# A two-layer graph kernel on one core: the half tile's first product dealt among the wide matmuls of the tile in front, and the unit numbers loaded three at a time

## The reference

```
x = x + C @ (D^-1/2 (sym(adj) + I) D^-1/2) @ layernorm(x)     # graph layer: C is adj too
h = layernorm(layernorm(x)) * gamma + beta                    # 2048 tokens of 512
shared = silu(h @ q(sw1).T) @ q(sw2).T                        # 512 -> 1024 -> 512
e, p = argmax and max of softmax(h @ router.T)                # one expert of 8 for each token
routed = p * (silu(h @ q(ew1[e]).T) @ q(ew2[e]).T)
x = x + shared + routed
```

## Time and profile before

| | |
|---|---|
| times of three runs | 663.97, 664.15, 666.87 us (median 664.15) |
| the profiled execution | 665.43 us, of which the span is 663.7 us |
| mean granted PE clock | 0.991 |
| PE busy | 615.6 us (93%), 4713 matmuls |
| DVE busy | 478.0 us (72%) |
| ACT busy | 371.7 us (56%) |
| POOL busy | 185.8 us (28%) |
| chain that ended last | PE 64%, DMA 13%, DVE 12%, issue 5%, ACT 4% |

### The profile page before, as it was taken

How to read it: one execution, slowest core, us unless ns; L and a number is a source line. 1 busy time by engine, 2 the same in 40 slices (tenths; PEclk the granted TensorE clock), 3 DMA queues, 4 the chain that set the end, 5 groups by cost and what they waited for, 6 DMA issues and landing times.

```text
span 663.7 us, 14071 instructions
## 1 busy us (share of the span) xinstructions
PE 615.6 (93%) x4713; PEld 348.9 (53%) x4713; DVE 478.0 (72%) x1075; ACT 371.7 (56%) x699; POOL 185.8 (28%) x222
## 2 busy tenths in 40 slices
PE   0689899999997999999997999999999999999994
PEld 0234344444443444444443467777766666676672
DVE  4888986777776655778866669887885677666764
ACT  1667756677887777688836513556633424334241
POOL 2234343322210100202232416100120544445432
PEclk9999999999999999999998999999999999999998
DMA  8999990795878888967675975998259589676651
GB/s 341 420 416 415 421 368 26 187 225 144 233 230 259 292 263 274 351 226 254 206 237 203 225 209 129 236 227 178 78 90 231 148 192 183 180 193 173 181 127 62
DMA packets 105971, 149.87 MB, mean 226 GB/s; under 512 B 64590, under 2 KB 64590, under 8 KB 101808
## 3 DMA queue, kind: packets, MB, share of 16 engines
q1 hardware_dynamic: 91280, 116.82, 58.5%
q0 software_dynamic: 7632, 23.23, 11.3%
q10 hardware_dynamic: 6992, 8.93, 4.5%
HBM read 117.73 MB, written 18.25 MB: 205 GB/s over the span
## 4 chain that ended last, share of the span: by engine, by line
PE 64%; DMA 13%; DVE 12%; issue 5%; ACT 4%; SPq 1%; POOL 1%; DVEq 0%; ACTq 0%; POOLq 0%
PE bank L1785 14%; PE bank L1813 13%; PE bank L1680 10%; PE bank L1678 10%; PE bank L1679 10%; DMA region<-in_adj_t 7%; DMA work<-in_w 3%; PE bank L1828 2%; ACT junk L940 2%; DVE region L1194 2%; PE bank L1842 1%; DMA hb<-h_scratch,zreg 1%; PE bank L1708 1%; DVE region L1190 1%; DVE work L1308 1%
## 5 line engine op out<-in xcount | busy, mean ns | idle before, releaser
L1813 PE MATMUL bank<-region,work 128*128 128x512 f16 (+1 forms) x512 | 116.8, 379 | 3.5 <-DVE work L1466 3.3
L1049 ACT ACTIVATE work<-work 128x512 f32<-128x512 f32 x64 | 39.8, 621 | 108.0 <-DVE work L1456 107.4
L1678 PE MATMUL bank<-region,work 128*128 128x512 f16 x192 | 73.7, 384 | 26.4 <-DVE region L1218 26.3
L1813 PEld LDWEIGHTS bank<-region,work 128*128 128x128 f16 x512 | 46.6, 98 | 61.3 <-issue 9.1
L1785 PE MATMUL bank<-zreg,region 128*128 128x128 f16 x1280 | 75.7, 219 | 0.0
L1785 PEld LDWEIGHTS bank<-zreg,region 128*128 128x128 f16 (+1 forms) x1280 | 72.7, 98 | 3.7 <-issue 0.2
L1679 PE MATMUL bank<-region,work 128*128 128x512 f16 x192 | 73.5, 383 | 0.0
L1680 PE MATMUL bank<-region,work 128*128 128x512 f16 x192 | 73.5, 383 | 0.0
L1678 PE MATMUL bank<-zreg,work 128*128 128x512 f16 x180 | 69.6, 386 | 0.0
L1680 PE MATMUL bank<-zreg,work 128*128 128x512 f16 x180 | 69.5, 386 | 0.0
L1679 PE MATMUL bank<-zreg,work 128*128 128x512 f16 x180 | 69.5, 386 | 0.0
(11 more groups left out here) (211 smaller groups left out, 1160.4 us busy)
## 6 DMA issues: line engine op xcount, KB each, us to landing
work<-in_w SPq DMA_DIRECT2D x46, 512.0 KB, 4.5
region<-in_adj SPq DMA_DIRECT2D x16, 1024.0 KB, 10.7
region<-in_adj_t SPq DMA_DIRECT2D x16, 1024.0 KB, 7.7
work<-in_adj_t SPq DMA_DIRECT2D x32, 384.0 KB, 4.4
region<-in_w SPq DMA_DIRECT2D x12, 512.0 KB, 4.2
xb<-in_w SPq DMA_DIRECT2D x10, 512.0 KB, 4.3
zreg<-s_scratch SPq DMA_DIRECT2D x17, 256.0 KB, 3.9
zreg<-in_x SPq DMA_DIRECT2D x4, 1024.0 KB, 9.7
```

What stands on the lines that cost most here:

```text
L1049: nc.scalar.activation(h1[:, cols], pre[:, cols], ACT.Silu).then_inc(h1_ok, 1)
L1678: nc.tensor.matmul(dst, a_hi, b_hi, start=start, stop=False, skip_group_check=True)
L1813: last = nc.tensor.matmul(ps_y[b][:, :].rearrange("p (d c) -> p d c", d=DB), h1hl[:, b, h, f * P:(f + 1) * P], w, start=(f == 0 and h == 0 ...
```

## The change

`first_of_half` goes. `half_beside(n, u, u_prior)` takes its place and does both the first product of the half tile n and the second product of the full tile n - 1 in front of it: four narrow matmuls, then one wide matmul ahead of each two narrow ones, 14 in all, and the last two wide ones after the last narrow one. The wait for the first half of tile n - 1 stands before the first wide matmul, that for its second half before the ninth. `m1_ok` of the half tile is raised by its last narrow matmul and `m2_ok` of tile n - 1 by the last wide one. The block of a second product is moved into `second_block`. Unit numbers are no longer loaded one for each tile: where n + 1 is a half tile, the second product of tile n - 1 loads three, those of n + 2 to n + 4, at f = 1, 3 and 5; the first second product of the stage loads two; the products of half tiles and `half_beside` load none. DVE, ACT, POOL and SP are as they were.

```
--- before.py
+++ after.py
@@ -60,6 +60,8 @@
 IDLE = 8
 MIXED = 4
 HALF_TILE = P // 2
+HALF_LEAD = 4
+HALF_SHARE = 2
 FULL_TILES = N // P
 HALF_TILES = E - 1
 ROUTED_TILES = FULL_TILES + HALF_TILES
@@ -1800,50 +1802,64 @@
                                                 start=(d == 0 and h == 0), stop=False, skip_group_check=True)
                 last.then_inc(r_ok, 1)
 
-            def second_product(n, u, ahead=None):
-                b, nxt = n % 2, None
+            def second_product(n, u, ahead=()):
+
+                units = []
                 pe.wait_ge(h1lo_ok, 2 * n + 2)
                 if n >= 2:
                     pe.wait_ge(y_ok, n - 1)
                 for f in range(FB):
-                    if f == FB // 4 and ahead is not None:
-                        nxt = load_unit(ahead)
-                    w = w2t[:, ds(u * (4 * CHUNK), 4 * CHUNK)].rearrange("p (d f c) -> p f d c", d=DB, f=FB)[:, f, :, :]
+                    if f % 2 and len(units) < len(ahead):
+                        units.append(load_unit(ahead[len(units)]))
                     for h in range(2):
-                        last = nc.tensor.matmul(ps_y[b][:, :].rearrange("p (d c) -> p d c", d=DB),
-                                                h1hl[:, b, h, f * P:(f + 1) * P], w,
-                                                start=(f == 0 and h == 0), stop=False, skip_group_check=True)
+                        last = second_block(n, u, f, h)
                 last.then_inc(m2_ok, 1)
-                return nxt
-
-            def first_of_half(n, u):
+                return units
+
+            def second_block(n, u, f, h):
 
                 b = n % 2
+                w = w2t[:, ds(u * (4 * CHUNK), 4 * CHUNK)].rearrange("p (d f c) -> p f d c", d=DB, f=FB)[:, f, :, :]
+                return nc.tensor.matmul(ps_y[b][:, :].rearrange("p (d c) -> p d c", d=DB),
+                                        h1hl[:, b, h, f * P:(f + 1) * P], w,
+                                        start=(f == 0 and h == 0), stop=False, skip_group_check=True)
+
+            def half_beside(n, u, u_prior):
+
+                b, dealt = n % 2, 0
                 columns_in(n)
                 pe.wait_ge(pre_ok, 2 * n - 2)
                 both = ht[n % RING].rearrange("p (h d t) -> p h d t", h=2, d=DB)
-                for f in range(FB):
-                    for d in range(DB):
-                        w = w1t[:, ds(u * (4 * CHUNK) + (f // 2) * CHUNK + d * 2 * P + (f % 2) * P, P)]
-                        last = nc.tensor.matmul(
-                            ps_h[b][f // 4][:, (f % 4) * P:(f % 4 + 1) * P].rearrange("p (h t) -> p h t", h=2), w,
-                            both[:, :, d, 0:HALF_TILE], start=(f % 4 == 0 and d == 0), stop=False, skip_group_check=True)
+                for i in range(FB * DB):
+                    if i >= HALF_LEAD and (i - HALF_LEAD) % HALF_SHARE == 0:
+                        if dealt == 0:
+                            pe.wait_ge(h1lo_ok, 2 * n - 1)
+                            pe.wait_ge(y_ok, n - 2)
+                        elif dealt == FB:
+                            pe.wait_ge(h1lo_ok, 2 * n)
+                        second_block(n - 1, u_prior, dealt // 2, dealt % 2)
+                        dealt += 1
+                    f, d = i // DB, i % DB
+                    w = w1t[:, ds(u * (4 * CHUNK) + (f // 2) * CHUNK + d * 2 * P + (f % 2) * P, P)]
+                    last = nc.tensor.matmul(
+                        ps_h[b][f // 4][:, (f % 4) * P:(f % 4 + 1) * P].rearrange("p (h t) -> p h t", h=2), w,
+                        both[:, :, d, 0:HALF_TILE], start=(f % 4 == 0 and d == 0), stop=False, skip_group_check=True)
                 last.then_inc(m1_ok, 1)
-
-            def second_of_half(n, u, ahead):
+                for i in range(dealt, 2 * FB):
+                    last = second_block(n - 1, u_prior, i // 2, i % 2)
+                last.then_inc(m2_ok, 1)
+
+            def second_of_half(n, u):
 
                 b = n % 2
                 pe.wait_ge(h1lo_ok, 2 * n + 2)
                 pe.wait_ge(y_ok, n - 1)
                 for f in range(FB):
-                    if f == FB // 4:
-                        nxt = load_unit(ahead)
                     w = w2t[:, ds(u * (4 * CHUNK), 4 * CHUNK)].rearrange("p (d f c) -> p f d c", d=DB, f=FB)[:, f, :, :]
                     last = nc.tensor.matmul(ps_y[b][:, :].rearrange("p (d c) -> p d c", d=DB),
                                             h1hl[:, b, 0, f * P:(f + 1) * P], w, start=f == 0, stop=False,
                                             skip_group_check=True)
                 last.then_inc(m2_ok, 1)
-                return nxt
 
             def load_unit(n):
                 return pe.value_load(unit[0:1, n:n + 1], min_val=0, max_val=UNITS - 1)
@@ -1901,18 +1917,20 @@
 
             pe.wait_ge(wt_ok, 2 * CHUNKS)
             pe.wait_ge(unit_ok, 1)
-            u, before_u = load_unit(NT), 0
+            units, u_prior = [load_unit(NT)], 0
             for n in range(NT, TILES):
+                u = units.pop(0)
                 if is_half(n):
-                    first_of_half(n, u)
+                    half_beside(n, u, u_prior)
                 else:
                     first_product(n, u)
-                if is_half(n - 1):
-                    nxt = second_of_half(n - 1, before_u, n + 1)
-                else:
-                    nxt = second_product(n - 1, before_u, n + 1 if n + 1 < TILES else None)
-                u, before_u = nxt, u
-            second_product(TILES - 1, before_u)
+                    if is_half(n - 1):
+                        second_of_half(n - 1, u_prior)
+                    else:
+                        ahead = range(n + 1, n + 3) if n == NT else range(n + 2, n + 5) if is_half(n + 1) else ()
+                        units += second_product(n - 1, u_prior, [t for t in ahead if t < TILES])
+                u_prior = u
+            second_product(TILES - 1, u_prior)
 
 
 def kernel(x, adj, L0_ffn_shared_w1, L0_ffn_shared_w2, L0_ffn_expert_w1, L0_ffn_expert_w2, L0_ffn_router_w,
```

## The result

Median of 17 runs 668.51 us (665.83 to 673.84), of the kernel before in 17 runs beside them 664.97. The ratio is 1.0052, with a 95% interval of 1.0033 to 1.0071. The profiled execution took 666.50 us with a span of 664.8. That single execution lies low: its part up to the routed tiles was 2.1 us faster than in the profile of before (the first routed matmul at 500.62 against 502.70). Where two traces are compared, I therefore compare the routed stage itself, from the first matmul of tile 16 to the last second product, that of tile 38: 652.82 - 502.70 = 150.1 us before, 653.88 - 500.62 = 153.3 after. The forecast was 3.5 more; this is 3.1.

What follows compares the result with a forecast made beforehand. PE, with its sequencer, bounds the kernel before; after, a loop through VectorE of 14.40 + 0.25 + 4.65 + 0.28 = 19.58 us against 19.15. With start and end, 664.15 + 3.5 = 667.6 us, range 660.5 to 670.5.

Steps and rivals of the forecast that it cites:

- The sequencer's sum: PE's sequencer over three routed tiles: 18.3 us after the change, for 17.6 of matmuls; period before 19.15.
- The unit loads gain or lose little: Three loads in one second product: 0.7 us each beside wide matmuls; only the first stops PE, by up to 0.3.
- The loop through VectorE: Routed tiles: the half tile's m1_ok comes after the mix, closing a loop of 19.58 us per three tiles, against 19.15.
- VectorE's part: VectorE's work in the loop, from half tile's start to the first half of the next mix's front tile: 14.40 us.
- VectorE to PE: From the end of VectorE's first half to PE's first wide matmul: 0.14 plus 0.1 for a second wait, 0.25 us.
- the mixed part: First wide to last narrow matmul in the mixed block: 4.65 us, bounds 4.54 and 4.9.
- the last narrow matmul to VectorE: From the mix's last narrow matmul to VectorE's start on the half tile: 0.28 us.
- Start and end: Routed stage's ends: first second product idles about 0.4 us (bounds 0 and 0.7); tile 38's second product at 656.3, before 652.82.
- The sum: Start, six loops of 19.58 us and end of the routed stage together: +3.5 us.
- PE alone counts: Rival 1, routed tiles: VectorE's queue gets out of the way, period 18.3, time 658.5 us; chance 0.20.
- Addresses computed twice: Rival 2, mixed block: 48 addresses, 0.9 us more a loop, time 673.0 us; rivals 2 to 4 together 0.11.
- The clock at tile 38: Rival 3: idle before tile 38's second product drops the clock to 1.2 GHz, doubling its 3.45: 671.0 us; rivals 2-4 together 0.11.

Runs made afterwards that it cites:

- `HALF_LEAD` 12: Changed kernel with twelve narrow matmuls, not 4, ahead of the first wide one: 661.09 us, ratio 0.9945 to the kernel before.
- `HALF_LEAD` 8: Changed kernel with eight narrow matmuls, not 4, ahead of the first wide one: 662.74 us, ratio 0.9976 to the kernel before.
- `HALF_LEAD` 20: Changed kernel with 20 narrow matmuls first, second-half wait ahead of the ninth wide one: 662.23 us, ratio 0.9969 to the kernel before.

## Why the prediction was right, step by step

**The sequencer's sum** (18.3 us for three tiles): right. It is the period of `HALF_LEAD` 12 (18.38), and halving the half tile's addresses moved its block in the kernel before from 2.61 to 1.82 us.

**The unit loads gain or lose little**: wrong, and hidden by the rest. The sentence was about the product that holds them, where it is true (0.17 of stop). But three loads there leave no lead for the block behind. With the half tile's product whole, that made 3.63 out of 2.61 us and a ratio of 1.0081. In the changed kernel it did not show, because PE waits for VectorE at that point anyway, and my sequencer's sum had counted it.

**The loop through VectorE** (19.58): right, with 19.44 measured. VectorE's part 14.40 came out at 14.38, VectorE to PE 0.25 at 0.14 (613.75 to 613.89; the second wait instruction, for which I had added 0.1, cost nothing), the mixed part 4.65 at 4.62, the last narrow matmul to VectorE 0.28 at 0.25. Taking work off VectorE or off the mixed part shortened the period by about that work (0.64 of an expected 0.66 at `HALF_LEAD` 8) until another bound was reached, and the same cut in the kernel before did nothing to its periods. The loop is shown, not only argued.

**Start and end.** The first second product stops 0.81 us, not 0.4, and above the bound of 0.7, which took a load at 0.7: this load was a slow one. In the five other traces that have the same loads there and no slow one, the product took 0 to 0.3 us more than its 3.45. The size of this term in the one trace is luck. The wait at tile 38 went to 2.29, foreseen 2.4.

**The sum** was +3.5 us. The stage shows 3.1, the medians 3.54 of 17 runs each. That they agree so well owes something to two errors of opposite sign: six periods 0.14 shorter than written (-0.8) and 0.4 more at the start, where a slow load happened to fall.

**Rivals.** PE alone counts (658.5): what spoke for it, VectorE's 13 busy of 19 us, was true and did not matter. It became true of the kernel at `HALF_LEAD` 12, once the loop was under the sum. Addresses computed twice: no, both traces hold 14071 instructions and 128 addresses for the wide matmuls of the stage, and the mixed part took 4.62 us. The clock at tile 38: it stayed at full in the profile of the changed kernel after 2.29 us of idle, and fell in that of `HALF_LEAD` 12 after 2.07, and there again, with the loads at f = 2, 4 and 6, after 2.04. Windows of the first trace at 12 (us, PE busy, then the other engines, granted clock third from the right):

```profile
644.50:646.50 2.00, 0.00 (x0) 0.00 (x0) 1.45 (x3) 1.10 (x2) 0.90 (x1) 1.00 0.45 82
646.50:648.50 2.00, 1.94 (x8) 0.91 (x9) 1.27 (x2) 0.00 (x0) 0.00 (x0) 0.83 0.24 94
648.50:650.50 2.00, 2.00 (x7) 0.66 (x5) 0.00 (x0) 0.00 (x0) 1.01 (x1) 0.50 0.12 45
```

```profile
646.56 5.31 PE L1823 MATMUL bank<-region,work 128*128 x16 [2.07 <-DVE work L1468]
```

```profile
646.18 5.31 PE L1823 MATMUL bank<-region,work 128*128 x16 [2.04 <-DVE work L1468]
```

The granted clock went to 1.2 GHz (0.50) after the idle, 1.3 us into the block in the first trace and at about its start in the second (a mean of 0.53 from 646.10 to 648.10). In both it was back at full before the block ended, and the block took 5.31 us instead of 3.62. So the rival can happen, and cost 1.7 us, not my 3.45, because only a part of the block ran at the lower clock. It happened in 2 of the 13 traces, with 0.7 to 2.3 us of idle ahead of that block in all of them. The changed kernel's runs scatter more (665.83 to 673.84, before 663.97 to 668.48 in as many), and those at a mean clock of 0.989 or less have a mean of 670.5 us, those at 0.993 or more 667.3. But the same split of the 75 runs of the kernel before that were taken beside the experiments gives 665.8 and 664.1, so this alone doesn't point to tile 38. How often the clock falls there in the changed kernel is not known, with one trace of it.

## What to carry to other kernels

When matmuls of one tile are dealt among those of another, list what the first wait in the mix now holds back: here the signal that ends the mix starts the engine for which its beginning waits, and that loop has a length of its own, which no busy share shows. Put enough work without a wait ahead of the first waiting instruction that the loop stays below the other bounds. And count the sequencer: where addresses come from a register, its lead, and what uses it up, decides which block is slow.

## What the runs showed of the hardware that was not expected

Matmuls with their weight loads cost PE's sequencer next to nothing: 32 addresses with one matmul each took as long (4.1 us, 534.7 to 538.8) as 32 with two (4.0, 547.7 to 551.7), some 130 ns an address. A load of a register from memory took 0.7 us of the sequencer in the earlier trace rows, with 0.31 for its first instruction. That instruction took about 0.30 in most loads of every trace, but 0.5 to 1.05 in one to four of them, at places that change from trace to trace. Where PE had no lead, such a load stopped it for up to 0.9 us. What makes a load slow was not found. Three of them (from 550.5 and 569.7 at `HALF_LEAD` 20 with half the addresses, from 598.6 in the kernel before with them) start within 1 us of the end of a wait of VectorE for late scale rows; whether the two have one cause was not tested. The sequencer was stopped with 18 matmuls issued and not started: by 541.7 seven addresses of tile 22 stand in the trace of the kernel before, 14 narrow matmuls, and 12 of the 16 wide ones ahead had started.

```profile
L1785 PEldq FUSED_REGOPS  x7: 46/46/46, 540.9 to 541.6; - x7
...
539.14 2.83 PE L1813 MATMUL bank<-region,work 128*128 x12
```

Ten wide matmuls in a row (2.2 us), as at `HALF_LEAD` 20, are already more lead than it can use for the narrow ones behind: their addresses took 4.6 us instead of 4.1.
